# Attention maxima of two heads at once, in the upper and lower half of the matmul array

## What is computed

```python
def _attn(q, k, v, mask=None):
    s = jnp.einsum('bhqd,bhkd->bhqk', q, k) / np.float32(np.sqrt(HD))
    if mask is not None:
        s = jnp.where(mask, s, jnp.float32(-1000000000.0))
    return jnp.einsum('bhqk,bhkd->bhqd', jax.nn.softmax(s, -1), v)
...
o1 = _attn(q, k1, v1, causal[None, None])       # all keys up to the query
...
o2 = _attn(q, ks, vs)                           # 256 selected tokens
...
o3 = _attn(q, kw, vw, winmask[None, None])      # a window of 64 tokens
g = gate[:, :, None, None, None]
o = g[:, 0] * o1 + g[:, 1] * o2 + g[:, 2] * o3
```

## Time and profile before

| | before |
|---|---|
| median of three runs | 2780.97 us |
| profiled execution | 2781.34 us |
| its span | 2779.4 us |
| TensorE busy | 2320.6 us, 83% |
| VectorE busy | 1628.3 us, 59% |
| ScalarE busy | 1266.2 us, 46% |
| GpSimd busy | 669.8 us, 24% |
| mean granted clock | 0.908 |

### The profile page before, as it was taken

One profiled execution on the slowest core, in us unless ns is written; L12 is line 12 of the kernel. 1 busy time (PEld: TensorE's weight loads), 2 busy tenths in 40 slices (PEclk: granted clock), 3 DMA queues, 4 the chain that ended last, 5 costly groups with the idle time before them and its releaser, 6 DMA issues. The chain is left out here.

```text
span 2779.4 us, 45396 instructions
## 1 busy us (share of the span) xinstructions
PE 2320.6 (83%) x16656; PEld 1545.5 (56%) x16656; DVE 1628.3 (59%) x3043; ACT 1266.2 (46%) x2777; POOL 669.8 (24%) x687
## 2 busy tenths in 40 slices
PE   5585858663999999999999999999999999601995
PEld 3464545442666666666666666566566666401884
DVE  4758575734466466466566576566565564450766
ACT  2354545440455555555455455555555555310442
POOL 0265656573011011011011011011010010145332
PEclk9697978765999999999999999999999999655997
DMA  2255555479547646556655565664664660611113
GB/s 97 97 219 184 216 187 201 172 269 226 126 93 146 132 101 139 122 118 131 127 121 122 120 136 114 136 129 104 137 137 96 138 130 10 158 39 47 48 53 110
DMA packets 222841, 360.53 MB, mean 130 GB/s; under 512 B 68794, under 2 KB 124701, under 8 KB 222240
## 3 DMA queue, kind: packets, MB, share of 16 engines
q1 hardware_dynamic: 216288, 348.43, 50.1%
q0 software_dynamic: 4320, 8.43, 0.9%
q10 hardware_dynamic: 2016, 0.77, 0.2%
HBM read 229.58 MB, written 126.56 MB: 128 GB/s over the span
## 5 line engine op out<-in xcount | busy, mean ns | idle before, releaser
L1370 ACT ACTIVATE prob<-ps 128x512 f32<-128x512 f32 (+5 forms) x1600 | 637.8, 441 | 665.8 <-PE ps L1325 656.3
L1434 DVE TENSOR_REDUCE maxima<-ps 128x1 f32<-128x512 f32 (+3 forms) x768 | 387.5, 547 | 291.4 <-PE ps L1250 147.0
L1344 PE MATMUL ps<-prob,plain 128*32 128x512 f32 (+5 forms) x3200 | 512.0, 443 | 0.0
L1400 POOL TENSOR_TENSOR products<-products,sums 128x256 f32<-128x256 f32 x192 | 140.8, 733 | 1540.3 <-DVE sums L1425 1539.0
L1439 DVE TENSOR_REDUCE maxima<-ps 128x2 f32<-128x512 f32 (+1 forms) x512 | 293.7, 606 | 192.6 <-PE ps L1261 98.4
L1425 DVE RECIPROCAL sums<-sums 128x256 f32<-128x256 f32 x192 | 331.9, 1736 | 97.6 <-ACT sums L1383 97.6
L1317 PE MATMUL ps<-q1a_s,k1a_s 128*128 128x512 f32 (+3 forms) x768 | 303.0, 395 | 0.0
L1325 PE MATMUL ps<-q1b_s,k1b_s 128*128 128x512 f32 (+3 forms) x768 | 301.1, 393 | 0.0
L1344 PE MATMUL ps<-prob,v_s 128*32 128x512 f32 (+3 forms) x1536 | 284.3, 491 | 0.0
L1250 PE MATMUL ps<-k1a_s,q1a_s 128*128 128x512 f32 (+3 forms) x768 | 234.5, 374 | 0.5 <-DVE maxima L1439 0.2
L1381 ACT ACTIVATE products<-ps,gates_a 64x512 f32<-64x512 f32 x192 | 131.0, 682 | 196.4 <-PE ps L1344 196.3
(11 more groups left out here) (333 smaller groups left out, 4889.8 us busy)
## 6 DMA issues: line engine op xcount, KB each, us to landing
qh_dram<-pairs SPq DMA_DIRECT2D x96, 512.0 KB, 2.7
kwh_dram<-pairs SPq DMA_DIRECT2D x64, 512.0 KB, 2.7
qa_s<-qh_dram SPq DMA_DIRECT2D x128, 256.0 KB, 4.7
kwa_s<-kwh_dram SPq DMA_DIRECT2D x128, 256.0 KB, 7.7
q1a_s<-qh_dram SPq DMA_DIRECT2D x128, 256.0 KB, 4.8
qb_s<-qh_dram SPq DMA_DIRECT2D x64, 256.0 KB, 9.3
kwb_s<-kwh_dram SPq DMA_DIRECT2D x64, 256.0 KB, 10.3
k1a_s<-k1ah_dram SPq DMA_DIRECT2D x32, 512.0 KB, 6.9
```

The costliest lines, as they stand in the source:

```text
L1344: mm = pe.matmul(ps[at:at + VD, SCORES + k % 2, q0 - c * CH:q0 - c * CH + w], w_, m.prob[:, n % PROBS, h, 0:w], start=first, stop=True, sk ...
L1370: act.activation(m.prob[:, u % PROBS, h, 0:w], ps[:, turn % SCORES, 0:w], ACT.Exp, scale=SCALE).then_inc(s["exp_done"], 1)
L1400: pool.tensor_tensor(o, o, m.sums[:, br, cc], ALU.mult).then_inc(s["divided"], 1)
L1434: ins = dve.tensor_reduce(partial[:, h, i, part:part + 1], bank[:, 0:w], AX, ALU.max)
```

## The change

The maxima of both heads are computed in one step. The queries of head 0 have their high parts in partitions 0 to 63 and their low parts in 64 to 127, those of head 1 the other way round. A maximum uses the high parts alone: 64 rows, head 0 in the upper half of the array (64*128), head 1 in the lower half, into two banks. Mask matmuls stay 128*128. A step takes two of four fill banks (SPARES = 4), and all sums share one bank, so the first products of a sum wait until the copies of the sum before are done. Products are grouped within a sum: (12) alone, (13, 14) ... (23, 24). The queries `qa` and `q1a` are loaded head by head, in eight DMAs instead of four.

```diff
+STARTS = [min(u for u, x in enumerate(UNITS) if x[:2] == k) for k in SUMS]
+TOGETHER = [tuple(range(u, min(u + 2, last + 1))) for first, last in zip(STARTS, LAST) for u in range(first, last + 1, 2)]
 SCORES = 3
-SPARES = 3
+SPARES = 4
...
-    max0 = [("max0", side, h, i, part) for h in range(HP) for i in range(NT) for part in range(1 + (i >= NT // 2))]
-    max1, max2 = [[(kind, side, h, k) for h in range(HP) for k in range(NT // 2)] for kind in ("max1", "max2")]
-    todo = max2 + max1[:3] + [("rows", side, 2)] + max1[3:] + max0[:3] + [("rows", side, 1)] + max0[3:]
+    max0 = [("max0", side, i, part) for i in range(NT) for part in range(1 + (i >= NT // 2))]
+    max1, max2 = [[(kind, side, k) for k in range(NT // 2)] for kind in ("max1", "max2")]
+    todo = max2 + max1[:2] + [("rows", side, 2)] + max1[2:] + max0[:2] + [("rows", side, 1)] + max0[2:]
...
-        ready = range(u - 2, u) if u >= 2 and u % 2 == 0 else range(u - 1, u) if u == len(UNITS) else ()
+        ready = [x for group in TOGETHER if group[-1] + 1 == u for x in group]
...
+    def upper_and_lower(first):
+
+        return [(h, at, comp + (lo ^ h)) for h in range(HP) for lo in range(2)
+                for at, comp in ((64 * lo, first), (64 * lo + 32, 4))]
...
-                for at, comp in ((0, 2), (32, 4), (64, 3), (96, 5)):
-                    sp.dma_start(m.qa[at:at + 32, k].bitcast(F32), two(src.q[g, comp], side)).then_inc(near, 16)
+                for h, at, comp in upper_and_lower(2):
+                    sp.dma_start(m.qa[at:at + 32, k, h].bitcast(F32), one(src.q[g, comp], side, h)).then_inc(near, 16)
...
-                if n >= SPARES:
-                    pe.wait_ge(s["emptied"], n - SPARES + 1)
-                bank, k = ps[:, 8 - SPARES + n % SPARES, :], side % 2
+                def bank(h):
+                    if n + h >= SPARES:
+                        pe.wait_ge(s["emptied"], n + h - SPARES + 1)
+                    return ps[:, 8 - SPARES + (n + h) % SPARES, :]
+
+                k = side % 2
+                upper = [slice(HD * h, HD * h + HD) for h in range(HP)]
                 if kind == "max0":
...
+                    both = [bank(h) for h in range(HP)]
+                    last = [pe.matmul(both[h][:, 0:k1 - k0], m.q1a[r, k, h, i * P:(i + 1) * P], m.k1a[r, k, k0:k1],
+                                      start=True, stop=True, skip_group_check=True) for h, r in enumerate(upper)]
                     if k1 == (i + 1) * P:
-                        mm = pe.matmul(bank[:, k1 - k0 - P:k1 - k0], m.ident_bf[:], m.causal_q[:],
-                                       start=False, stop=True, skip_group_check=True)
+                        last = [pe.matmul(both[h][:, k1 - k0 - P:k1 - k0], m.ident_bf[:], m.causal_q[:],
+                                          start=False, stop=True, skip_group_check=True) for h in range(HP)]
+                    for mm in last:
+                        mm.then_inc(s["fill_ready"], 1)
...
-                if first and k >= 2:
-                    pe.wait_ge(s["banks_free"], k - 1)
+                if first and k >= 1:
+                    pe.wait_ge(s["banks_free"], k)
...
-                        mm = pe.matmul(ps[at:at + VD, SCORES + k % 2, q0 - c * CH:q0 - c * CH + w], w_,
+                        mm = pe.matmul(ps[at:at + VD, SCORES, q0 - c * CH:q0 - c * CH + w], w_,
```

More of the change, by code:

```diff
@@ L1071, in __init__ @@
         self.steps = steps
-        self.fills = self.of(("max0", "max1", "max2", "rows", "proj"))
-        self.fill_no = {x: n for n, x in enumerate(self.fills)}
+        self.fills = [x for x in steps if x[0] in ("rows", "proj")
+                      or x[0] in ("max0", "max1", "max2") for h in range(self.banks(x))]
+        self.fill_no = {x: self.fills.index(x) for x in set(self.fills)}
         self.divisions = {x: n + 1 for n, x in enumerate(self.of(("divide",)))}
@@ L1078, in of, with banks @@
         return [x for x in self.steps if x[0] in kinds]
+    def banks(self, step):
+        return HP if step[0] in ("max0", "max1", "max2") else 1
 PLAN = Plan()
@@ L1140, in turn_no, with one @@
         return side // 2 + 1
+    def one(x, side, h):
+        return x[HP * NOPE * (side % 2) + NOPE * h:HP * NOPE * (side % 2) + NOPE * (h + 1)]
+    def upper_and_lower(first):
+        return [(h, at, comp + (lo ^ h)) for h in range(HP) for lo in range(2)
+                for at, comp in ((64 * lo, first), (64 * lo + 32, 4))]
     with nc.Block() as block:
@@ L1171, in whole @@
                 far, late = s["far%d" % k], s["late%d" % k]
-                for at, comp in ((0, 0), (32, 4), (64, 1), (96, 5)):
-                    sp.dma_start(m.q1a[at:at + 32, k].bitcast(F32), two(src.q[g, comp], side)).then_inc(far, 16)
+                for h, at, comp in upper_and_lower(0):
+                    sp.dma_start(m.q1a[at:at + 32, k, h].bitcast(F32), one(src.q[g, comp], side, h)).then_inc(far, 16)
                 sp.dma_start(m.k1a[:, k].bitcast(F32), src.k1a).then_inc(far, 16)
@@ L1255, in fill @@
                 elif kind == "max1":
-                    h, pair = a
                     once("near%d" % k, 16 * NEAR * turn_no(side))
                     once("keys%d" % k, 16 * KEYS * turn_no(side))
+                    both = [bank(h) for h in range(HP)]
                     for i in range(2):
-                        t = 2 * pair + i
-                        mm = pe.matmul(bank[:, i * KEEP:(i + 1) * KEEP], m.qa[:, k, h, t * P:(t + 1) * P],
-                                       m.ksa[:, k, h, :], start=True, stop=True)
+                        t = 2 * a[0] + i
+                        for h, r in enumerate(upper):
+                            mm = pe.matmul(both[h][:, i * KEEP:(i + 1) * KEEP], m.qa[r, k, h, t * P:(t + 1) * P],
+                                           m.ksa[r, k, h, :], start=True, stop=True, skip_group_check=True)
+                            if i == 1:
+                                mm.then_inc(s["fill_ready"], 1)
@@ L1263, in fill @@
                 elif kind == "max2":
-                    h, pair = a
                     once("consts", 16 * len(consts))
                     once("near%d" % k, 16 * NEAR * turn_no(side))
+                    both = [bank(h) for h in range(HP)]
                     for i in range(2):
-                        t = 2 * pair + i
+                        t = 2 * a[0] + i
                         k0 = max(0, t * P - WINDOW)
[L1270 to L1274, removed]
+                        for h, r in enumerate(upper):
+                            pe.matmul(both[h][:, i * KEEP:i * KEEP + WN], m.qa[r, k, h, t * P:(t + 1) * P],
+                                      m.kwa[r, k, h, k0:k0 + WN], start=True, stop=True, skip_group_check=True)
@@ L1275, in fill @@
+                    for h in range(HP):
+                        for i in range(2):
+                            mm = pe.matmul(both[h][:, i * KEEP:i * KEEP + WN], m.ident_bf[:],
+                                           m.window_q0[:] if 2 * a[0] + i == 0 else m.window_q[:], start=False, stop=True,
+                                           skip_group_check=True)
+                        mm.then_inc(s["fill_ready"], 1)
                 elif kind == "rows":
@@ L1285, in fill @@
                     pe.wait_ge(s["o_done"], PIECES * (NC * (side // 2) + c + 1))
-                    pe.matmul(bank, m.wvp[:, g], m.products[:, 0, cc], start=True, stop=False)
-                    mm = pe.matmul(bank, m.wproj[:, g], m.products[:, 1, cc], start=False, stop=True)
-                mm.then_inc(s["fill_ready"], 1)
+                    room = bank(0)
+                    pe.matmul(room, m.wvp[:, g], m.products[:, 0, cc], start=True, stop=False)
+                    pe.matmul(room, m.wproj[:, g], m.products[:, 1, cc], start=False, stop=True)\
+                        .then_inc(s["fill_ready"], 1)
             def scores(side, u):
@@ L1427, in _ @@
                     continue
[L1428 to L1442, removed]
+                for h in range(plan.banks(step)):
+                    n = plan.fill_no[step] + h
+                    bank = ps[:, 8 - SPARES + n % SPARES, :]
+                    dve.wait_ge(s["fill_ready"], n + 1)
+                    if kind == "max0":
+                        _, _, i, part = step
+                        w = min((part + 1) * CH, (i + 1) * P) - part * CH
+                        dve.tensor_reduce(partial[:, h, i, part:part + 1], bank[:, 0:w], AX, ALU.max)\
+                            .then_inc(s["emptied"], 1)
+                    elif kind in ("max1", "max2"):
+                        w = KEEP if kind == "max1" else WN
+                        at = h * NT + 2 * step[2]
+                        dve.tensor_reduce(negs[1 if kind == "max1" else 2][:, at:at + 2],
+                                          bank.rearrange("p (i n) -> p i n", i=2)[:, :, 0:w], AX, ALU.max,
+                                          negate=True).then_inc(s["emptied"], 1)
+                if plan.banks(step) > 1:
```

(2 more changed lines are left out.)

12 lines of the change are left out of this document (5 added, 7 removed).

## The result

The kernel after takes 2841.46 us (median of four runs), against 2781.91 for before in the same comparison: a ratio of 1.021, 95% interval 1.0192 to 1.0228. It is slower by 59.5 us. The forecast was 2837, 56 us slower.

The account below looks back on a forecast made before the run. TensorE was taken to bound the kernel, with array form changes deciding: 31 x (0.65 pauses net of streams + 0.2 grouping + 0.9 waits) + 2 at the start = 56 us on 2781.3, so 2837; range 2800 to 2898.

Parts of the forecast that it names:

- The bound: Attention: TensorE, 97.8% busy, sets the time of a side, 52.8 us; 1 us a side changes the kernel by about 31.
- The pause of a form change: TensorE entering or leaving the 64-row form: 0.10 us of emptying plus the weights, 0.20 us in and 0.20 out.
- The saved streams are within it; about +0.65: Maxima steps: form-change pauses outweigh the 3.41 us of stream saved a side, net about +0.65 us a side.
- pairs within a sum, +0.2: Products: one group more a side adds form changes of 0.13 and 0.20, less about 0.13 of weight waits: +0.2 us.
- Waits, +0.9: TensorE's waits on ScalarE: unit 15's new wait and shifts at units 4, 8, 10 and 19, +0.9 us a side.
- unit 15: TensorE at unit 15 needs the exponential of unit 14's first head before ScalarE hands it over: new wait of 0.5 us.
- One bank for products, 0: First products of a sum: waiting for the previous sum's copies on ScalarE is met already by an exponential's wait: 0.
- DMAs, 0 in the period: SyncE queue: 8 more issues a side, 3.5 us, hidden by the queue's own waits; without that cover 3.5 us a side.
- start: Start of attention: first row of maxima behind 12 more DMA issues, 0 to 5.3 us, taken as +2.
- Loads of the halves are not one after the other: Denies the rival that weights of the two halves load one after the other: +130 us, 2910; chance 0.12.
- streams are not either: Denies the rival that the two halves' streams run one after the other, no gain: +160 us, 2940; chance 0.05.
- the pause does not vanish: Denies the rival that halves need no pause: -1.9 us a side, 2722 us, faster, below 2775; chance 0.08.

Follow-up runs that it names:

- groups within sums alone: The kernel before with only the products grouped within a sum (12 alone, then 13 and 14, to 23 and 24): 2817.47 us, ratio 1.0116.
- the same, four and one banks: groups within sums alone, plus four banks for fills and one for products, fills still single over all 128 rows: 2807.27 us, ratio 1.0091.
- after, maxima over all rows: The kernel after with the maxima over all 128 rows again, still two heads a step: 2817.87 us, ratio 1.0133 to before.
- the kernel with three banks: The kernel after with three banks for fills and two for products, as in before: 3011.20 us, ratio 1.0818 to before.
- the kernel with single fills in one half: The kernel before with each single fill in the 64-row form, upper half alone, nothing side by side: 3067.45 us, ratio 1.1033.

## Why the prediction was right, and where its terms were off

The mechanism was the forecast one, and the nearness of the total (56 against 59.5) is in part luck: errors of the terms cancel.

**The bound** held. TensorE's sequence sets the time of a side: 1.90 us a side (unrounded 1.907) times 30 is 57.2 of 59.5.

To compare the terms, the time of a side is parted in two, by starts and streams as in the prediction and over all 30 periods: gaps of over 0.26 us between one stream and the next (waits, with a pause of 0.20 within some), and the rest (streams, pauses, short waits for weights). These are estimates.

| kernel | us a side | gaps over 0.26 | rest |
|---|---|---|---|
| before | 52.81 | 2.28 | 50.53 |
| groups within sums alone | 53.83 | 3.00 | 50.83 |
| the same, four and one banks | 53.60 | 3.01 | 50.59 |
| after, maxima over all rows | 53.95 | 4.03 | 49.92 |
| after | 54.71 | 3.48 | 51.23 |

**The pause of a form change** held, and it is the cause of the halves' part. Shown three ways: in after's timeline (0.10 us and the weights, into the halves, into the masks); by taking it away (all rows, 23.6 us faster although it streams more); by adding 76 of them a side with nothing else (9.1 us a side). The last two agree at 0.12 us net a change. The rule of the Trainium skill (TensorEngine Tiling (Array Packing), Key Properties) that a mode change drains agrees with these. Its other half, that tiles load and multiply in parallel, is now shown too, by two loads in 0.19 us.

**"The saved streams are within it; about +0.65"** and **pairs within a sum, +0.2** make up the rest: 0.85 was forecast, 51.23 - 50.53 = 0.70 came. **Waits, +0.9:** 3.48 - 2.28 = +1.2 came. The errors, -0.15 and +0.3, cancel in part. The new wait at unit 15 (0.56) and the shifts at units 4, 8 and 10 (from 0.44 in every second side, 0.39 and 0.64 to 0.86 in every second side, 0.86 and 0.26: +0.3 a side) together are what the +0.9 was made of. The rest of the +1.2, 0.3 a side, is the wait before the projection, which comes twice in two sides: 1.36 and 0.71 before, 1.43 and 1.29 after. The forecast has no term for it.

The halves alone, against all rows: the rest grows by 1.31, and 0.55 of the waits goes, since pauses cover it; +0.76 is what is left.

**Unit 15.** The new wait of 0.5 us came where it was worked out, and nearly as large: L1356 at 1494.02 is recorded 0.08 longer than usual and streams until 1494.21, L1348 at 1494.66 streams from 1494.77 after its weights: 0.56 us. It is in the run with all rows too (0.57), and not with groups alone: it needs two heads in one step, and whether it needs the groups as well was not run.

**Pairs within a sum** cost 1.02 when they are made alone. The +0.2 is their two form changes, and the rest, 50.83 - 50.53 = 0.3, bears it out. The other 0.7 is waits, forecast as waits for exponentials and found as fills that wait for VectorE behind a division. In after no fill waits so; other waits stand in their place. So the parts don't add up by themselves: 1.02, -0.23, +0.35, +0.76 are the steps in one order of adding, and another order would divide 1.90 otherwise.

**One bank for products, 0**, and **DMAs, 0 in the period**, held as far as the traces show: in after no gap of over 0.26 us in the 30 periods ends with a DMA or with the copies of a sum. No run took the loads head by head away. SyncE's queue still waits for products 592.7 us, against 699.6. The **start** was forecast at +2 for longer queues: TensorE waited 10.78 us for the first row of maxima instead of 8.79,

```profile
697.11 0.80 PE L1348 MATMUL ps<-qa_s,ksa_s 128*128 128x512 f32 x1 [10.78 <-DMA qb_s<-mrows]
```

but the first maxima were done 3.2 us earlier (685.7 against 688.9), so scores began 1.3 us earlier than in before. The second mark is at 750.4 in both: 0 instead of +2. Why the first maxima came earlier is open. The last side brought 2.3 that was not forecast; that the two are nearly equal is luck.

**The rivals.** Loads of the halves are not one after the other (two in 0.19 us), streams are not either, and the pause does not vanish. The speed-up of up to 2 that the Trainium skill gives (TensorEngine Tiling (Array Packing), Theoretical Speedup) is true here of the stream of a pair alone; the best place seen, eight matmuls of selected keys, takes 0.67 us instead of 0.96.

Open: the +0.35 for two heads in a step over all rows is +1.0 of waits and -0.7 of the rest, by the table. Which part of the edit brings the waits (fills in twos, or their place between the scores) was not taken apart.

## What to carry over

Price a change of the array's form before using a part of the array: here it was 0.20 us each way with float32 weights, so a pair of heads between score matmuls had to save more than 0.40 us of stream, which 512 columns (0.21) never do. It can pay only where several such steps stand together or where a form change stands anyway. Count what an order of groups does to the other engines' queues, even if it touches no instruction. And ask first whether an operation is needed: the masks in the maxima were worth more than the whole rearrangement, in the other direction.

## What the runs showed of the hardware that was not expected

The granted clock fell to the lower level behind waits of TensorE of up to 1.5 us (0.50 to 0.57 in the stretches behind one of them, 0.97 over the attention part of the kernel with three banks), while after, with waits of up to about 1.4 us, kept 1.00. It fell as well where TensorE had no such wait and was recorded busy without a break: 0.61 over 8 us in the kernel with single fills in one half, behind fills that each changed the form. So neither the longest wait nor the recorded busy share says by itself whether the clock stays; where the limit lies is open.

Two matmuls of 512 columns into the two halves and two different banks, with float32r operands, take 0.50 us together, as one alone takes that waits for its weights.
